# A two-layer block with disentangled attention: SyncE's order of writes and reads of the skewed tables, and tables made 20 slots ahead

## The chip, the cores and the metric

The kernel runs on one core of one Trainium2 chip, as one program. The metric is the device time of one execution in microseconds; the median of the runs counts. TensorE (PE), VectorE (DVE), ScalarE (ACT), GpSimd (POOL) and SyncE (SP) each run their own instruction stream and meet through semaphores. In this kernel SyncE computes nothing; it issues DMAs in the order in which they are written for it.

## The reference

Input x has the shape (4, 1024, 256), float32. Two layers follow each other, each added to its own input after a layer norm:

```
x = x + LN(attention(LN(x)))
x = x + LN(experts(LN(x)))
```

The attention has 16 heads of width 16 and relative positions. With a bucketed distance rel(q, k), clipped to 128 buckets:

```
scores[q,k] = (Q[q].K[k] + Q[q].posK[c2p(q-k)] + K[k].posK[p2c(q-k)]) / sqrt(48)
out = LN(softmax(scores) @ V @ Wo + bo + hidden)
```

The buckets are such that only distances below 128 have a table value of their own; from 128 on, all keys to one side share one value. The second layer sends each token to one of 8 experts (256 to 1024 to 256, ReLU), adding the other experts' constant outputs.

## The kernel before

Five stages run one after the other: `spread` (position tables), `project` (norm, Q, K, V), `attend`, `mix` (output projection, norms, routing) and `experts`. Only `attend` is touched; it takes the time from about 200 us to 1492 us of the span.

**Units and slots.** `attend` works on N = 64 units, one for each batch entry and head. A unit has QT = 8 row tiles of 128 queries; the work on one tile is a slot, counted by s from 0 to 511. All engines walk through the same slots in software-pipelined loops written out by hand; `AHEAD` (16 slots) and `LAG` (13 slots) say how far the first and the last part of a tile's work stand from the score.

**Tables.** For tile x, 16 slots ahead, TensorE's `make_table` (L703) multiplies queries and keys with the head's bucket rows into `table_ps`, a single PSUM buffer; ScalarE's `keep_table` (L852) copies it to `table`. Four tiles make a part (h = 0 for tiles 0 to 3, h = 1 for tiles 4 to 7). SyncE's `skew_write` (L650) writes a part to DRAM (1024 KB), and `skew_read` (L658) reads it back with a row pitch one element shorter, in two DMAs, one for each table (384 KB each for h = 0, 640 KB each for h = 1), so that the value for a distance comes to stand at its key: the tile `near`. The write waits until the fourth table is kept (`table_kept`) and until the reads of the unit two before have landed, as both use the same place in DRAM. The read waits for the landing of its write (`skew_out`) and until the scores of the unit two before have used `near` (`scored`, `seen`).

**Corners.** GpSimd's `edge` (L916) makes the two corner blocks of `near` in five operations for each h (L926, L929, L934, L939, L942), spread over the slots by the tuple `steps` (L964): each entry is (slot in relation to the unit before, h, operations). The last one raises `near_made`. `keep_side` (L910) first copies the last column of the table, which two of the operations use. GpSimd works through its list in order; a wait holds all that stands behind.

**Scores.** TensorE's `score` (L717) makes a 128 x 1024 tile of scores, waits for `near_made`, and adds `near` by transposes (L740). It waits for VectorE's `seen` of two slots ago. VectorE's `look` (L807) takes the maxima and writes the band around the diagonal, `level` (L828, L833) subtracts the running maximum.

**The unit's maximum.** After slot 7 of a unit GpSimd's `split_top` (L947) splits the row maxima in five small operations (L952 to L962); TensorE's `turn_top` (L782, L785), at slot 1 of the next unit, waits for them and turns them into `table_ps`; ScalarE's `keep_top` sends them by DMA to the query tile. The next but one `make_table` waits for `top_kept`.

**The rest of the slot.** 13 slots behind the score, TensorE's `flip` makes the transposed scores in two halves, ScalarE's `exponent` (L865) the exponential, TensorE's `weigh` (L767) the sum with the values.

**SyncE's iteration.** In iteration u of its loop (L677 to L695) SyncE issues, in this order: read(u+1, h=1), write(u+2, h=0), `load_unit(u+4)` (queries and keys in five DMAs, which wait for the flips of unit u-2), store(u-2), read(u+2, h=0), write(u+2, h=1). A batch of values (1152 KB) is loaded at the start and in iterations 4, 20 and 36.

Of the kernel before, what the change touches and what calls it, by code (L numbers as in the profile page):

```python
# [16 lines left out]
P = 128  # L17
# [4 lines left out]
N = B * H  # L22
QT = S // P
# [7 lines left out]
BAND = 2 * P - 1  # L31
# [522 lines left out]

def attend(nc, sem, spent, c_masks, split_d, far_d, v_d, pick_d, skew_d, ctx_d):

    AHEAD = 2 * QT
    LAG = QT + 5
    BUFS = 6
    HATS = 5  # L560
# [13 lines left out]
    with ExitStack() as ctx:  # L574
# [10 lines left out]
        rows = sb("rows", [KROWS, H, 2, 2 * P], BF16)  # L585
        vals = [sb(f"vals{i}", [P, QT, VROW]) for i in range(2)]
        table = [sb(f"table{i}", [P, 2, 2, 4, SPOT]) for i in range(2)]
        side = [sb(f"side{i}", [P, 2, QT]) for i in range(2)]
        near = [sb(f"near{i}", [P, 2, QT, W3]) for i in range(2)]
        band = [sb(f"band{i}", [P, QT, W3]) for i in range(2)]  # L590
        most, peak = sb("most", [P, 2, 2]), sb("peak", [P, 2, 2])
# [36 lines left out]
        @block.sync  # L628
        def _(sp):
            part, far = N * DH * S, PARTS * S  # L630

            def load_unit(n):
                i = n % BUFS
                if n >= BUFS:
                    sp.wait_ge(flipped, 2 * QT * (n - BUFS + 1))
                for dst, side_at in ((after[i], TERMS * part), (quest[i], 0)):
                    sp.dma_start(dst[0:KROWS, :], view(split_d, side_at + n * (DH * S), [[part, TERMS], [S, DH], [1, S]])
                                 ).then_inc(hats_in[i], 16)
                for dst, far_at, many in ((quest[i][FAR:FAR + 6, :], n * (2 * far), 2 * PARTS),
                                          (after[i][KROWS:FAR, :], (N + n) * (2 * far) + far, PARTS),  # L640
                                          (before[i][KROWS:FAR, :], (N + n) * (2 * far), PARTS)):
                    sp.dma_start(dst, view(far_d, far_at, [[S, many], [1, S]])).then_inc(hats_in[i], 16)

            def load_vals(b):
                if b >= 2:
                    sp.wait_ge(summed, QT * BATCH * (b - 1))
                sp.dma_start(vals[b % 2][:, :, :], view(v_d, b * (S * VROW), [[VROW, P], [P * VROW, QT], [1, VROW]])
                             ).then_inc(vals_in[b % 2], 16)

            def skew_write(n, h):  # L650
                sp.wait_ge(table_kept, n * QT + 4 * h + 4)
                if n >= 2:
                    sp.wait_ge(skew_in[n % 2][0], 16 * 2 * (n // 2))
                    sp.wait_ge(skew_in[n % 2][1], 16 * 2 * (n // 2))
                sp.dma_start(view(skew_d, n % 2 * (P * PITCH) + h * 4 * SPOT + 1, [[PITCH, P], [TABLE, 2], [1, 4 * SPOT]]),
                             table[n % 2][:, h, :, :, :].rearrange("p a u v -> p a (u v)")).then_inc(skew_out[n % 2][h], 16)

            def skew_read(n, h):  # L658
                if n >= 2:
                    sp.wait_ge(scored, (n - 2) * QT + 4 * h + 4)  # L660
                    sp.wait_ge(seen, (n - 2) * QT + 4 * h + 4)
                sp.wait_ge(skew_out[n % 2][h], 16 * (n // 2 + 1))
                lo, hi = PIECES[h]
                for tab in range(2):
                    sp.dma_start(near[n % 2][:, tab, lo:hi, P:W3],
                                 view(skew_d, n % 2 * (P * PITCH) + tab * TABLE + lo * SPOT + P,
                                      [[PITCH - 1, P], [SPOT, hi - lo], [1, SPOT]])).then_inc(skew_in[n % 2][h], 16)

            def store(n):
                sp.wait_ge(sum_kept, n + 1)  # L670
                sp.dma_start(view(ctx_d, n * (P * 2 * P), [[2 * P, P], [1, 2 * P]]), made[n % 2][:, :]
                             ).then_inc(ctx_out[n % 2], 16)

            for semaphore in spent:
                sp.sem_clear(semaphore)
            sp.dma_start(rows[:, :, :, :].rearrange("p h a v -> p (h a v)"), pick_d[:, :]).then_inc(rows_in, 16)
            for u in range(-4, N + 3):  # L677
                if 0 <= u + 1 < N:
                    skew_read(u + 1, 1)
                if 0 <= u + 2 < N:  # L680
                    skew_write(u + 2, 0)
                if 0 <= u + 4 < N:
                    load_unit(u + 4)
                if u == -4:
                    sp.dma_start(masks[:, :, :], c_masks).then_inc(const_in, 16)
                if 0 <= u - 2 < N:
                    store(u - 2)
                if u == -4:
                    load_vals(0)
                if u % BATCH == 4 and u // BATCH + 1 < B:  # L690
                    load_vals(u // BATCH + 1)
                if 0 <= u + 2 < N:
                    skew_read(u + 2, 0)
                if 0 <= u + 2 < N:
                    skew_write(u + 2, 1)  # L695
            for i in range(2):
                sp.wait_ge(ctx_out[i], 16 * (N // 2))

        @block.tensor
        def _(pe):  # L700
            ident = masks[:, 4, :]

            def make_table(x):  # L703
                n, u = x // QT, x % QT
                i = n % BUFS
                if u == 0:
                    pe.wait_ge(hats_in[i], 16 * HATS * (n // BUFS + 1))
                if x >= 1:
                    pe.wait_ge(table_kept, x)
                if x >= AHEAD and x % QT == 2:  # L710
                    pe.wait_ge(top_kept, (x - AHEAD) // QT)
                nc.tensor.matmul(table_ps[:, 0, :], quest[i][0:KROWS, u * P:(u + 1) * P], rows[:, n % H, 0, :],  # L712
                                 start=True, stop=False)
                nc.tensor.matmul(table_ps[:, 1, :], after[i][0:KROWS, u * P:(u + 1) * P], rows[:, n % H, 1, :],  # L714
                                 start=False, stop=True).then_inc(table_made, 1)
# [193 lines left out]
        def _(pool):  # L909
            def keep_side(n, h):  # L910
                pool.wait_ge(table_kept, n * QT + 4 * h + 4)
                if n >= 2:
                    pool.wait_ge(edge_made, (n - 2) * 10 + (5 if h == 0 else 10))
                nc.gpsimd.tensor_copy(side[n % 2][:, :, 4 * h:4 * h + 4], table[n % 2][:, h, :, :, BAND]).then_inc(side_kept, 1)

            def edge(n, h, step):  # L916
                i = n % 2
# [6 lines left out]
                if step == 0:  # L924
                    pool.wait_ge(skew_in[i][h], 16 * 2 * (n // 2 + 1))
                    nc.gpsimd.tensor_tensor(head[:, 0, :, :], tail[:, 0, :, :], above, ALU.mult).then_inc(edge_made, 1)  # L926
                elif step == 1:
                    pool.wait_ge(side_kept, n * 2 + h + 1)
                    nc.gpsimd.tensor_tensor(head[:, 1, :, :], tail[:, 1, :, :],  # L929
                                            side[i][:, 1, lo + 1:hi + 1].unsqueeze(2).to_broadcast([P, many, P]),  # L930
                                            ALU.subtract).then_inc(edge_made, 1)
                elif step == 2:
                    pool.wait_ge(edge_made, done + 1)
                    nc.gpsimd.tensor_tensor(tail[:, 0, :, :], tail[:, 0, :, :],  # L934
                                            side[i][:, 0, lo:hi].unsqueeze(2).to_broadcast([P, many, P]),
                                            ALU.subtract).then_inc(edge_made, 1)
                elif step == 3:
                    pool.wait_ge(edge_made, done + 2)
                    nc.gpsimd.tensor_tensor(head[:, 1, :, :], head[:, 1, :, :], above, ALU.mult).then_inc(edge_made, 1)  # L939
                else:  # L940
                    pool.wait_ge(edge_made, done + 3)
                    nc.gpsimd.tensor_tensor(tail, tail, masks[:, 1, :].unsqueeze(1).unsqueeze(1).to_broadcast([P, 2, many, P]),  # L942
                                            ALU.mult).then_inc(edge_made, 1)
                    pool.wait_ge(edge_made, done + 5)
                    pool.sem_inc(near_made, 1)  # L945

            def split_top(n):  # L947
                i, done = n % 2, 5 * n
                if n >= 2:
# [11 lines left out]
                pool.wait_ge(split_made, done + 4)  # L961
                nc.gpsimd.tensor_copy(top_part[i][:, 2, :], top_rest[:, 1, :]).then_inc(split_made, 1)  # L962

            steps = ((2, 0, (0, 1)), (3, 0, (2,)), (4, 0, (3,)), (5, 0, (4,)),  # L964
                     (6, 1, (0, 1)), (7, 1, (2,)), (8, 1, (3,)), (9, 1, (4,)))
            nc.gpsimd.memset(before_rows[:, :], -1.0).then_inc(before_set, 1)
            pool.wait_ge(before_set, 1)
            nc.gpsimd.memset(before_rows[0:6, :], 0.0).then_inc(before_set, 1)
# [2 lines left out]
            pool.wait_ge(const_in, 16)  # L971
            for s in range(-AHEAD, TS):
                u, t = s // QT, s % QT
                if t == 0 and 0 <= u + 1 < N:
                    keep_side(u + 1, 1)
                if t == 4 and 0 <= u + 2 < N:
                    keep_side(u + 2, 0)
                for at, h, of in steps:
                    n = (s - at) // QT + 1
                    if (s - at) % QT == 0 and 0 <= n < N:  # L980
# [659 lines left out]
```

## Time and profile before

| | us |
|---|---|
| median of 3 runs | 2009.08 (2002.75 to 2014.89) |
| the profiled execution | 2003.63 |
| its span, from the first to the last instruction | 2001.7 |
| PE busy / PEld busy | 1698.0 / 1159.6 |
| DVE busy | 1370.7 |
| ACT busy | 1121.8 |
| POOL busy | 1069.1 |
| DMA, mean over the span | 226 GB/s |

The busy times are unions of an engine's instructions. PE is TensorE's matmuls, whose ends are modelled, so that a busy PE is not one at its peak; PEld is its weight loads, which run beside them. A time in brackets behind an instruction is how long its engine stood idle before it, with what ended the idle time.

### The profile page before, as it was taken

The page shows a single profiled execution, that of the slowest core. Times are in us where ns is not written, and L with a number is a line of the kernel's source. Part 1 is how long each engine was busy: PE and PEld are TensorE (multiplying, and loading weights), DVE is VectorE, ACT ScalarE, POOL GpSimd, SP SyncE. Part 2 cuts the span into 40 slices and gives each one's busy share as a digit, 9 for nine tenths or more (in the row PEclk, how much of TensorE's full clock was granted, in tenths as well). Part 3 has the DMA queues.
Part 4 walks back from the last instruction along what each step waited for, and adds up shares of the span by engine and source line. Part 5 has one row for each costly group of instructions (what it writes and reads, how often), then busy time and mean ns, then how long its engine had stood idle before and what let it go on. Part 6 is the DMA issues. An engine that isn't in the chain of part 4 may idle for free. (4 is left out here: it accounts for less than half of the span.)

```text
span 2001.7 us, 40568 instructions
## 1 busy us (share of the span) xinstructions
PE 1698.0 (85%) x13688; PEld 1159.6 (58%) x13688; DVE 1370.7 (68%) x3938; ACT 1121.8 (56%) x2233; POOL 1069.1 (53%) x1268
## 2 busy tenths in 40 slices
PE   1882389999999999999999999999973674999997
PEld 1451156565656566566565666566532464999996
DVE  1673188788888788898798899899843553343343
ACT  1672257676767677677677777677751460222221
POOL 0210267676777667667576777777711451233332
PEclk6996589999999999999999999999996675999998
DMA  4598778777777777777877777787718852676772
GB/s 113 188 303 274 225 250 262 246 237 251 245 261 248 256 247 240 257 254 245 265 237 251 249 261 250 240 272 246 235 44 215 284 176 86 198 212 215 223 219 78
DMA packets 320826, 453.36 MB, mean 226 GB/s; under 512 B 35132, under 2 KB 260303, under 8 KB 320526
## 3 DMA queue, kind: packets, MB, share of 16 engines
q1 hardware_dynamic: 308034, 415.25, 65.2%
q10 hardware_dynamic: 7596, 21.10, 3.4%
q0 software_dynamic: 4992, 14.43, 1.9%
q8 instruction: 112, 1.84, 0.4%
q14 instruction: 92, 0.75, 0.1%
HBM read 257.32 MB, written 193.65 MB: 225 GB/s over the span
## 5 line engine op out<-in xcount | busy, mean ns | idle before, releaser
L865 ACT ACTIVATE t_probsT<-t_flip 128x512 f32<-128x512 f32 x1024 | 619.2, 607 | 242.7 <-PE t_flip L756 117.5
L814 DVE TENSOR_REDUCE t_most<-t_scores 128x1 f32<-128x640 f32 (+1 forms) x512 | 436.7, 853 | 169.8 <-PE t_scores L740 166.5
L833 DVE TENSOR_SCALAR t_band<-t_band,t_top 128x384 f32<-128x384 f32 (+1 forms) x512 | 383.8, 750 | 0.0
L859 ACT COPY t_table<-t_table_ps 128x512 f32<-128x512 f32 x512 | 298.2, 582 | 70.7 <-issue 41.1
L777 PE MATMUL t_sum_ps<-t_probsT,t_vals 128*32 128x256 f32 x4096 | 329.5, 394 | 0.2 <-ACT t_probsT L865 0.2
L926 POOL TENSOR_TENSOR t_near<-t_near,t_masks 128x384 f32<-128x384 f32 (+1 forms) x128 | 146.8, 1147 | 338.9 <-DMA t_near<-skew_d 336.4
L942 POOL TENSOR_TENSOR t_near<-t_near,t_masks 128x768 f32<-128x768 f32 (+1 forms) x128 | 272.4, 2129 | 0.0
L763 PE MATMUL t_flip<-t_masks,t_band 128*128 128x128 f32 x1408 | 263.0, 276 | 0.0
L818 DVE CUSTOM_DVE_ANT_0 t_band<-t_scores,t_near 128x384 f32<-128x384 f32 (+1 forms) x512 | 262.1, 512 | 0.0
L740 PE MATMUL t_scores<-t_masks,t_near 128*128 128x128 f32 x1408 | 243.5, 277 | 7.1 <-POOLq L945 7.1
L733 PE MATMUL t_scores<-t_after,t_quest 105*128 105x256 bf16 (+3 forms) x1024 | 244.9, 289 | 2.6 <-DVE t_most L818 2.4
L740 PEld LDWEIGHTS t_scores<-t_masks,t_near 128*128 128x128 f32 x1408 | 182.7, 143 | 46.6 <-POOLq L945 8.7
L712 PE MATMUL t_table_ps<-t_rows,t_quest 96*128 96x256 bf16 x512 | 143.5, 280 | 69.1 <-DMA t_before<-far_d 49.8
L733 PE MATMUL t_scores<-t_before,t_quest 105*128 105x256 bf16 (+3 forms) x768 | 195.0, 294 | 0.0
L763 PEld LDWEIGHTS t_flip<-t_masks,t_band 128*128 128x128 f32 x1408 | 164.7, 143 | 4.8
L756 PE MATMUL t_flip<-t_quest,t_before 108*128 108x512 bf16 (+3 forms) x512 | 161.4, 316 | 0.8 <-ACT t_probsT L865 0.7
L756 PE MATMUL t_flip<-t_quest,t_after 108*128 108x512 bf16 (+3 forms) x512 | 158.7, 310 | 1.2 <-DMA t_quest<-t_topT 0.8
L1606 PE MATMUL e_hid_ps<-e_xT,e_w 128*128 128x128 f32 x1248 | 148.0, 278 | 5.6 <-DMA e_total<-total_d 5.2
L1606 PEld LDWEIGHTS e_hid_ps<-e_xT,e_w 128*128 128x128 f32 x1248 | 147.5, 194 | 8.2 <-issue 5.5
L939 POOL TENSOR_TENSOR t_near<-t_near,t_masks 128x384 f32<-128x384 f32 (+1 forms) x128 | 145.5, 1137 | 0.0
L714 PE MATMUL t_table_ps<-t_rows,t_after 96*128 96x256 bf16 x512 | 142.9, 279 | 0.0
L1588 PE MATMUL e_out_ps<-w_all,e_hid 128*128 x624 | 141.0, 379 | 0.0
(186 smaller groups left out, 2343.7 us busy)
## 6 DMA issues: line engine op xcount, KB each, us to landing
skew_d<-t_table SPq DMA_DIRECT2D x128, 1024.0 KB, 8.9
t_near<-skew_d SPq DMA_DIRECT2D x128, 640.0 KB, 6.2
t_near<-skew_d SPq DMA_DIRECT2D x128, 384.0 KB, 4.8
e_w<-in_L_ffn_W_dram ACTq DMA_DIRECT2D x39, 512.0 KB
e_w<-in_L_ffn_W_dram SPq DMA_DIRECT2D x39, 512.0 KB
split_d<-p_part SPq DMA_DIRECT2D x32, 384.0 KB
t_after<-split_d SPq DMA_DIRECT2D x64, 192.0 KB
t_quest<-split_d SPq DMA_DIRECT2D x64, 192.0 KB
```

The lines of the kernel that those rows point to most:

```text
L733: nc.tensor.matmul(out[:, at:at + size], quest[i][0:XROWS, t * P:(t + 1) * P], keys[0:XROWS, piece[0] * P:piece[0] * P + size], start=at % ...
L740: last = nc.tensor.matmul(out[:, (j - lo) * P:(j - lo + 1) * P], near[n % 2][:, 1, j, (t - j + 1) * P:(t - j + 2) * P], ident, start=False ...
L756: last = nc.tensor.matmul(out[:, (a - lo) * P:(z - lo) * P], keys[:, j * P:(j + 1) * P], quest[i][:, a * P:z * P], start=first, stop=False ...
L763: last = nc.tensor.matmul(out[:, (t - lo) * P:(t - lo + 1) * P], band[n % 2][:, t, at:at + P], ident, start=False, stop=True, is_transpose ...
L777: last = nc.tensor.matmul(sum_ps[32 * g:32 * g + 32, 0:2 * P], vals[b % 2][:, j, h * VDIM:h * VDIM + 32], probsT[s % 3][:, g * 2 * P:(g + ...
L814: nc.vector.tensor_reduce(most[:, c, 1:2], out[:, wide:S], AX.X, ALU.max)
L818: nc.vector.tensor_tensor_reduce(band[n % 2][:, t, 0:wide], out[:, 0:wide], near[n % 2][:, 0, t, at:at + wide], 1.0, -3.0e38, ALU.add, ALU ...
L833: nc.vector.tensor_scalar(band[n % 2][:, t, 0:wide], band[n % 2][:, t, 0:wide], top[n % 2][:, t:t + 1], None, ALU.subtract).then_inc(level ...
L859: nc.scalar.copy(table[n % 2][:, h, :, u % 4, :], table_ps[:, :, :]).then_inc(table_kept, 1)
L865: nc.scalar.activation(probsT[s % 3][:, half * 512:(half + 1) * 512], flip_ps[half][:, :], ACT.Exp, scale=SCALE).then_inc(expd, 1)
L942: nc.gpsimd.tensor_tensor(tail, tail, masks[:, 1, :].unsqueeze(1).unsqueeze(1).to_broadcast([P, 2, many, P]), ALU.mult).then_inc(edge_made, 1)
L1606: last = nc.tensor.matmul(hid_ps[s % 2][:, c, :], w1[s % WB][:, f, c * P:(c + 1) * P], xT[s % 2][:, f, :], start=(f == 0), stop=(f == 1))
```

## The change

Five edits, all in `attend`:

- SyncE's iteration has a new order: write(u+2, h=0), read(u+1, h=1), `load_unit(u+4)`, write(u+2, h=1), read(u+2, h=0), store(u-2), values.
- `AHEAD` is 20 slots instead of 16, on all engines. TensorE's wait for `top_kept` is kept at the same slot of the unit.
- `side` has three buffers instead of two, and `keep_side` waits for the edges of the unit three before.
- `keep_side` runs four slots earlier in relation to the unit whose column it copies: (u+2, h=0) at slot 0, (u+2, h=1) at slot 4.
- GpSimd's `steps` put each operation of h = 0 and the first three of h = 1 one slot earlier; the fourth and fifth of h = 1 stay at slots 0 and 1 of the next unit and now stand first in a slot.

```diff
-    AHEAD = 2 * QT
+    AHEAD = 2 * QT + QT // 2
...
-        side = [sb(f"side{i}", [P, 2, QT]) for i in range(2)]
+        side = [sb(f"side{i}", [P, 2, QT]) for i in range(3)]
...
             for u in range(-4, N + 3):
+                if 0 <= u + 2 < N:
+                    skew_write(u + 2, 0)
                 if 0 <= u + 1 < N:
                     skew_read(u + 1, 1)
-                if 0 <= u + 2 < N:
-                    skew_write(u + 2, 0)
                 if 0 <= u + 4 < N:
                     load_unit(u + 4)
                 if u == -4:
                     sp.dma_start(masks[:, :, :], c_masks).then_inc(const_in, 16)
+                    load_vals(0)
+                if 0 <= u + 2 < N:
+                    skew_write(u + 2, 1)
+                    skew_read(u + 2, 0)
                 if 0 <= u - 2 < N:
                     store(u - 2)
-                if u == -4:
-                    load_vals(0)
                 if u % BATCH == 4 and u // BATCH + 1 < B:
                     load_vals(u // BATCH + 1)
-                if 0 <= u + 2 < N:
-                    skew_read(u + 2, 0)
-                if 0 <= u + 2 < N:
-                    skew_write(u + 2, 1)
...
-                if x >= AHEAD and x % QT == 2:
+                if x >= AHEAD and (x - AHEAD) % QT == 2:
                     pe.wait_ge(top_kept, (x - AHEAD) // QT)
...
-                if n >= 2:
-                    pool.wait_ge(edge_made, (n - 2) * 10 + (5 if h == 0 else 10))
-                nc.gpsimd.tensor_copy(side[n % 2][:, :, 4 * h:4 * h + 4], table[n % 2][:, h, :, :, BAND]).then_inc(side_kept, 1)
+                if n >= 3:
+                    pool.wait_ge(edge_made, (n - 3) * 10 + 10)
+                nc.gpsimd.tensor_copy(side[n % 3][:, :, 4 * h:4 * h + 4], table[n % 2][:, h, :, :, BAND]).then_inc(side_kept, 1)
...
-            steps = ((2, 0, (0, 1)), (3, 0, (2,)), (4, 0, (3,)), (5, 0, (4,)),
-                     (6, 1, (0, 1)), (7, 1, (2,)), (8, 1, (3,)), (9, 1, (4,)))
+            steps = ((8, 1, (3,)), (9, 1, (4,)), (1, 0, (0, 1)), (2, 0, (2,)), (3, 0, (3,)), (4, 0, (4,)),
+                     (5, 1, (0, 1)), (6, 1, (2,)))
...
-                if t == 0 and 0 <= u + 1 < N:
-                    keep_side(u + 1, 1)
+                if t == 0 and 0 <= u + 2 < N:
+                    keep_side(u + 2, 0)
                 if t == 4 and 0 <= u + 2 < N:
-                    keep_side(u + 2, 0)
+                    keep_side(u + 2, 1)
```

## Rows read from the trace of the kernel before

**Rows 1.** The page, in 40 slices of the span: PE busy tenths, granted clock in tenths.
```profile
PE   1882389999999999999999999999973674999997
...
PEclk6996589999999999999999999999996675999998
```
**Rows 2.** Stretches: length; busy us of PE, PEld, DVE, ACT, POOL; clock; DMA share, GB/s.
```profile
284.50:1440.80 1156.30, 1103.46 (x10137) 694.85 (x10137) 1005.05 (x2881) 841.51 (x1618) 824.56 (x1022) 0.99 0.77 251
1310.40:1346.70 36.30, 36.02 (x343) 22.95 (x338) 33.21 (x98) 28.08 (x54) 26.95 (x35) 1.00 0.78 259
1440.80:1458.40 17.60, 16.63 (x154) 9.83 (x154) 16.56 (x48) 10.34 (x19) 13.60 (x17) 1.00 0.52 177
```
**Rows 3.** Timeline at two turns (L785): start, us, instruction, idle time before it.
```profile
1346.68 0.22 PE L785 MATMUL t_table_ps<-t_ident,t_top_part 128*24 128x128 bf16 x1
...
1458.40 0.23 PE L785 MATMUL t_table_ps<-t_ident,t_top_part 128*24 128x128 bf16 x1 [0.77 <-POOL t_top_part L962]
```
**Rows 4.** TensorE's waits, 284.5 to 1440.8 us: us in total, times, longest.
```profile
PE t_table_ps L785 <- POOL t_top_part L962: 46.3, 46, 4.4
```
**Rows 5.** Timeline of POOL and PE around one late turn; one stretch's clock.
```profile
804.56 1.28 POOL L926 TENSOR_TENSOR t_near<-t_near,t_masks 128x512 f32<-128x512 f32 x1 [5.68 <-DMA t_near<-skew_d]
807.84 0.19 POOL L952 CAST t_top_part<-t_top 128x8 bf16<-128x8 f32 x1
808.91 0.19 POOL L962 CAST t_top_part<-t_top_rest 128x8 bf16<-128x8 f32 x1
809.15 0.23 PE L785 MATMUL t_table_ps<-t_ident,t_top_part 128*24 128x128 bf16 x1 [1.64 <-POOL t_top_part L962]
809.30:812.60 3.30, 3.19 (x19) 2.27 (x22) 0.07 (x1) 1.83 (x4) 3.30 (x2) 0.61 0.86 244
```
**Rows 6.** Timeline of SyncE's queue over one unit.
```profile
1344.78 1.25 SPq L665 DMA_DIRECT2D t_near<-skew_d  x2
1346.13 0.57 SPq L655 DMA_DIRECT2D skew_d<-t_table  x1
1352.66 0.93 SPq L665 DMA_DIRECT2D t_near<-skew_d  x2
1353.69 0.56 SPq L655 DMA_DIRECT2D skew_d<-t_table  x1
...
1357.67 0.36 SPq L671 DMA_DIRECT2D ctx_d<-t_made  x1
1364.10 0.92 SPq L665 DMA_DIRECT2D t_near<-skew_d  x2
```
**Rows 7.** SyncE's own waits, 284.5 to 1440.8 us.
```profile
SPq L662 <- DMA skew_d<-t_table: 702.1, 116, 8.3
```
**Rows 8.** Time to landing of the writes (L655), then of the reads (L665).
```profile
DMA to landing us min/median/max: 5.7/8.9/10.9
...
DMA to landing us min/median/max: 3.7/5.3/8.5
```
**Rows 9.** Timeline of DVE and POOL in the two clean units.
```profile
1327.32 0.35 DVE L833 TENSOR_SCALAR t_band<-t_band,t_top 128x256 f32<-128x256 f32 x1
1329.30 2.37 POOL L942 TENSOR_TENSOR t_near<-t_near,t_masks 128x1024 f32<-128x1024 f32 x1
1329.58 2.23 DVE L833 TENSOR_SCALAR t_band<-t_band,t_top 128x256 f32<-128x256 f32 x1
1343.32 0.08 DVE L825 DVE_READ_ACCUMULATOR t_peak<-t_most 128x1 f32 x1
```
**Rows 10.** Timeline of the start: a table copy, slot 3's wait, the first turn.
```profile
234.81 0.58 ACT L859 COPY t_table<-t_table_ps 128x512 f32<-128x512 f32 x1 [0.70 <-PE t_table_ps L714]
249.27 0.90 PE L740 MATMUL t_scores<-t_masks,t_near 128*128 128x128 f32 x3 [6.90 <-POOLq L945]
265.71 0.28 PE L785 MATMUL t_table_ps<-t_ident,t_top_part 128*24 128x128 bf16 x1 [4.83 <-POOL t_top_part L962]
```
**Rows 11.** DVE's groups, 284.5 to 1440.8 us: busy us, mean ns.
```profile
L833 DVE TENSOR_SCALAR t_band<-t_band,t_top 128x256 f32<-128x256 f32 x480 | 362.0, 754 | 0.0
```

More of the change, by code:

```diff
@@ L929, in edge @@
                     nc.gpsimd.tensor_tensor(head[:, 1, :, :], tail[:, 1, :, :],
-                                            side[i][:, 1, lo + 1:hi + 1].unsqueeze(2).to_broadcast([P, many, P]),
+                                            side[n % 3][:, 1, lo + 1:hi + 1].unsqueeze(2).to_broadcast([P, many, P]),
                                             ALU.subtract).then_inc(edge_made, 1)
@@ L934, in edge @@
                     nc.gpsimd.tensor_tensor(tail[:, 0, :, :], tail[:, 0, :, :],
-                                            side[i][:, 0, lo:hi].unsqueeze(2).to_broadcast([P, many, P]),
+                                            side[n % 3][:, 0, lo:hi].unsqueeze(2).to_broadcast([P, many, P]),
                                             ALU.subtract).then_inc(edge_made, 1)
```

## The prediction

> **What bounds the kernel now.** I read the page's busy shares first [rows 1]. The attention stage runs from about 200 to 1492 us, and there the matmul row sits at nine tenths with a granted clock of nine tenths or more. An average says little here, so I next took one number per unit: the turn of the row maxima (`turn_top`, L785) happens once in each of the 64 units, first at 265.71 us [rows 10]. From the second turn to the 62nd (284.5 to 1440.8) are 60 pitches in 1156.30 us, a mean of 19.27 us [rows 2]. From the turn at 1310.4 to that at 1346.7 are two pitches in 36.30 us, at a full clock, with TensorE busy for 36.02 of them [rows 2], and the turn that ends them shows no idle time before it [rows 3]. So about 18.16 us is what TensorE's own work costs per unit, and about 1.11 us per unit is something else. A slot (one row tile of one head, eight to a unit) is 18.16 / 8 = 2.27 us of it.
>
> The list of waits says what the rest is: before L785 the matmuls waited 46.3 us in 46 places for GpSimd's L962, the last of the five small operations of `split_top` [rows 4]. That is 0.77 us per unit. The rest is a slower clock after such waits: TensorE is busy 1103.46 / 60 = 18.39 us per unit against 18.01 in the two clean ones [rows 2], 0.38 us. Together 1.15 of the 1.11 us. One such place, read across engines [rows 5]: GpSimd sat idle 5.68 us until a read of the skewed table landed, started L926 at 804.56, needed 3.28 us for the three operations ahead of `split_top` and 1.26 us for `split_top`, and TensorE turned at 809.15 after 1.64 us of idleness. After that idle time the granted clock was 0.61 on average from 809.3 to 812.6, so for the greater part its lower level (1.2 GHz) [rows 5]. Both costs are in the 19.27.
>
> Why is the read late? SyncE's queue, over a unit [rows 6]: reads at 1344.78, write at 1346.13, then nothing until 1352.66, reads, write at 1353.69, loads and store to 1358.03, then nothing until 1364.10. Each gap is the wait of the next read for the write just issued. SyncE waited 702.1 us for it in 116 places [rows 7], 11.7 us of each unit. The two round trips in series, 1344.78 to 1364.10, are 19.32 us: they pace the unit, and TensorE is caught by them through GpSimd. A write lands 8.9 us after issue in the median (5.7 to 10.9), a read 5.3 (3.7 to 8.5) [rows 8]. Bandwidth is not what is short: the DMA share is 0.77 at 19.27 us [rows 2].
>
> **The change part by part.** *Order on SyncE and tables 20 slots ahead.* I count in slots from the start of unit u. Before, `skew_write(u+2, 1)` was issued only when SyncE came free at the end of the iteration, and the read of it straight after its landing. Now the two writes of a unit are about half a unit ahead of their reads, with the other write between. The iteration runs: write(u+2,0) at about slot -0.3, when its fourth table is kept; read(u+1,1), after `seen` of unit u-1 (slot 0.7) and the landing of write(u+1,1); `load_unit(u+4)`, which must wait for the flips of unit u-2, slot 4.4 (they run 13 slots late); write(u+2,1); read(u+2,0); store. The wait in `load_unit` is not new, but the write now stands behind it and its five issues. The one chain that can still bind goes from there: on the queue the five loads of `load_unit` take from 1354.25, the end of the write's issue, to 1357.67, 3.4 us [rows 6], the write lands after 8.9, the reads land 8.5 after issue (the largest landing of before, since they now follow a 1 MB write) [rows 8], GpSimd needs 3.28 + 1.26 us [rows 5] until TensorE may turn. That sums to 25.4 us. The turn it feeds stands at slot 18, 13.6 slots after slot 4.4, which at 2.27 us is 30.9 us. So 5.5 us are spare. With the largest write (10.9) and a read longer by another 2.7 us, it is 30.1, still inside. The value batches (1152 KB, three of them in the loop) cost some of that in three units only.
>
> As a rule on the same thing: the Trainium skill, "DMA: Bandwidth & Descriptors", section "Queues, rings and completion order", says that within a queue each DMA engine takes descriptors in ring order. By it a read issued behind a write moves its bytes after it, and reads take longer to land than before while writes take less; the trace of before has the opposite order and fits (write 8.9, read 5.3) [rows 8]. Without the rule one would keep 5.3 for the read, and the spare time would be 8.7 us.
>
> *GpSimd's steps.* The eleven kinds of operation stay as they are, and their number too; 13.7 us of GpSimd per unit (824.56 / 60) [rows 2]. At slot 6 it now does h1's third operation and at slot 7 nothing but `split_top`, so `split_top` starts when slot 7's maximum is there. In the clean unit that maximum was ready at 1343.40 (L825) and the turn stood at 1346.68 [rows 3, 9]: 3.28 us for 1.26 us of work, 2.0 us spare. Behind `split_top` on GpSimd stand the side copy, two h1 operations (L939, taken like L926 at 1.28, and L942 at 2.37 us) [rows 5, 9] and then the h0 chain; h1's `near_made` comes at about 1.26 + 0.2 + 3.65 = 5.1 us after the maximum, some 4 us before slot 3's transposes ask for it. The h0 chain ends near slot 5.5, h1's first three near slot 7.0; GpSimd then idles 18.16 - 13.7 = 4.4 us. Sides in three buffers cost nothing but memory; the operation is the same, and its wait on `edge_made` is for work a unit old.
>
> *Steady gain.* 60 pitches x (19.27 - 18.16) = 66.6 us. The return of the clock is in it, since the two clean pitches are at full clock. The floor may not be held every time: bounds 0 and 0.3 us per unit (the latter a quarter of today's stall); I take 0.06, near the zero that the two adjacent clean units show: -4 us.
>
> *Start.* TensorE makes 20 tables before the first score instead of 16. Each is a round between TensorE and ScalarE of 0.70 + 0.58 = 1.28 us [rows 10], so the first score comes 5.1 us later. But today slot 3 of unit 0 waits 6.90 us for `near_made` of h1 (L740), and the first turn 4.83 us for GpSimd [rows 10]. The 5.1 us lie inside the 6.90. The read that slot 3 waits for no longer waits for read(0,0) to be issued, yet goes behind write(1,0): between -5 and +5 us, I take +1.5. The first turn's 4.83 us goes, as its read has half a unit more. Together 6.3, bounds -5.2 and 11.7.
>
> *End.* The wait of 0.77 us at 1458.40 goes [rows 3]. Four more of the late slots are free of tables; without tables the unit took 17.60 - 0.77 = 16.83 instead of 18.16 [rows 2, 3], so 4 x 0.16 = 0.65. Together 1.4. All other stages are untouched.
>
> Sum: 66.6 - 4 + 6.3 + 1.4 = 70.3 us. The profiled execution took 2003.63 us (span 2001.7): 2003.63 - 70.3 = 1933.3. The median of the three timed runs is 5.4 us above the profiled one; part of that is the scatter of the very stalls that go, so I leave it out of the point and put it in the range.
>
> **The rivals.** *VectorE takes over.* L833 took 0.35 us alone, but 2.23 us where it started during GpSimd's L942 (1329.30 to 1331.67); it ended at 1331.81, just behind it [rows 9]. Its mean is 0.754 [rows 11], so about 0.35 x 8 = 2.8 us of VectorE's 16.75 us per unit (1005.05 / 60) is this waiting. The spare is 18.16 - 16.75 = 1.4 us. GpSimd's operations move against VectorE's slots, so the waiting may grow; if by two thirds, the unit needs 18.64 us and, with slots uneven, about 18.7: 0.54 x 60 = 32 us of the gain is lost, 1966 us. Against it: neither engine has more to do, and in the clean units VectorE was busy 33.21 of 36.30 us without holding TensorE [rows 2]. The Trainium skill has this as a rule, "SBUF — State Buffer", section "Who interferes with whom": a VectorE instruction in a two-port mode and a GpSimd one exclude each other for the whole instruction. The trace agrees in the 2.23 us above.
>
> *The write behind the loads binds (slower).* The chain above must be done in 13.6 slots, so the pitch is at least chain / 1.7. From 32.8 us on, 7.4 more than my sum, the kernel is slower than now. If each of the three transfers in it takes 2.9 us more because three are in the queue at a time, the chain is 34 us, the pitch 20.0, and the time 2003.6 + 60 x 0.73 - 6 = 2041 us. For it: the DMA share must rise to 0.77 x 19.27 / 18.16 = 0.82. Against: the sum of worst landings stays under 31.
>
> *It does not do what it says.* Should GpSimd still start late, because the reads follow a whole write and come at the same point of the unit as now, the pitch stays at 19.27 and only start and end move: about 1998 us, inside 0.5%.
>
> **How the numbers follow.** 0.5% is 10 us, about what a measurement of this kernel can tell from no change. My forecast 0.68, with its own range 1924 to 1948; VectorE 0.18; no effect 0.06; slower 0.08. All of the first two are faster by over 0.5%, and a bit of the third: 0.87. Same 0.06, slower 0.07. The range of 8 in 10: 1923 (no residue, best start) to 1968 (VectorE's case).
>
> **What would show it.** L785's wait for L962 gone or below 5 us in all; pitches of 18.1 to 18.3 us from turn to turn; no stretch of the stage at the lower clock after the first unit; SyncE's wait at L662 for the write reduced to a few us per unit with a new one at L637 for the flips; L665 landing later than 5.3 us, L655 earlier than 8.9; GpSimd idle before L952 (waiting for the maximum) instead of before L926. Wrong, if L740 or L785 waits for GpSimd again, if L814 never waits for scores (VectorE full), or if the first turn is later than 265.7 us.

## The result, and the profile after

The changed kernel takes 1931.18 us in the median of 4 runs (1928.36 to 1933.84), against 2009.65 us (2002.75 to 2014.89): the ratio is 0.9611, 95% interval 0.9579 to 0.9644. The forecast was 1933.0 with a range of 1923 to 1968. The profiled execution took 1933.84 us, span 1931.9, so 69.8 us of span have gone.

The page's slices and the stretches come first, with the columns of [rows 1, 2]. The lines of the file have moved: L785 is now L783, GpSimd's L952 is L950, L962 is L960, L926 is L924, L740 is L738.

```profile
PE   1883289999999999999999999999944774999997
...
PEclk6897579999999999999999999999976665999999
```

```profile
281.50:1370.30 1088.80, 1080.11 (x10132) 687.90 (x10128) 1003.36 (x2879) 839.70 (x1614) 831.15 (x1020) 1.00 0.85 265
1370.30:1931.90 561.60, 443.93 (x2918) 381.24 (x2913) 238.54 (x818) 163.10 (x445) 183.40 (x187) 0.84 0.58 175
```

The first stretch is again from the second turn to the 62nd: 60 pitches in 1088.80 us where there were 1156.30 [rows 2]. All but two of them are 18.16 or 18.17 us, one is 18.37, and the last, without tables, is 16.88. The granted clock is 1.00 instead of 0.99, so the returns to 1.2 GHz that followed the waits [rows 5] are gone too. The second stretch is all that follows; before, it took 560.9 us from the 62nd turn. The 69.8 us are made up of 3.0 before the second turn (284.5 to 281.5), 67.5 in the pitches, and -0.7 behind them. Between the two medians lie 78.5 us; the kernel before scattered over 12.1 us in its four runs, the changed one over 5.5.

Next the waits of all engines from 277 to 1372 us (total, times, longest); these lines answer to [rows 4].

```profile
POOL t_top_part L950 <- DVE t_peak L823: 209.0, 60, 4.1
PEld t_flip L754 <- ACT t_probsT L863: 115.8, 302, 0.4
...
DVE t_most L812 <- PE t_scores L738: 66.9, 203, 0.4
...
POOL t_near L924 <- DMA t_near<-skew_d: 14.1, 11, 3.9
...
PEld t_flip L754 <- DMA t_quest<-t_topT: 2.3, 5, 0.6
...
PEld t_table_ps L783 <- POOL t_top_part L960: 0.2, 1, 0.2
```

GpSimd now waits for the maximum, 3.5 us per unit. Its wait for the read of the table, which had held it 5.68 us in the unit of [rows 5], is down to 14.1 us in 11 places. The turn waits for nobody, but for 0.2 us before one weight load. SyncE's own waits over the whole run follow, which answer to [rows 7], and then the landing times of the writes and of the reads [rows 8].

```profile
SPq L637 <- PE t_flip L761: 423.1, 58, 7.7
...
SPq L662 <- DVE t_most L816: 54.8, 51, 5.2
...
SPq L662 <- DMA skew_d<-t_table: 19.9, 15, 5.3
```

```profile
DMA to landing us min/median/max: 5.3/7.5/12.6
...
DMA to landing us min/median/max: 4.6/7.9/14.5
```

The wait of a read for its write fell from 702.1 us to 19.9. Reads now land later (7.9 against 5.3) and writes sooner (7.5 against 8.9), and neither shows up before the turn. Last, the timeline of SyncE's queue and of GpSimd over one unit, with the turn that ends it:

```profile
1304.92 0.76 SPq L637 DMA_DIRECT2D t_after<-split_d  x1
...
1307.72 0.56 SPq L655 DMA_DIRECT2D skew_d<-t_table  x1
1308.40 1.64 SPq L665 DMA_DIRECT2D t_near<-skew_d  x2
1310.08 1.28 SPq L671 DMA_DIRECT2D ctx_d<-t_made  x1
1312.34 0.56 SPq L655 DMA_DIRECT2D skew_d<-t_table  x1
1314.04 1.78 SPq L665 DMA_DIRECT2D t_near<-skew_d  x2
...
1325.01 1.29 POOL L924 TENSOR_TENSOR t_near<-t_near,t_masks 128x512 f32<-128x512 f32 x1 [0.22 <-DMA t_near<-skew_d]
1327.25 1.16 POOL L932 TENSOR_TENSOR t_near<-t_near,t_side 128x512 f32<-128x512 f32 x1
1332.52 0.25 POOL L950 CAST t_top_part<-t_top 128x8 bf16<-128x8 f32 x1 [4.11 <-DVE t_peak L823]
1333.66 0.19 POOL L960 CAST t_top_part<-t_top_rest 128x8 bf16<-128x8 f32 x1
1335.28 0.22 PE L783 MATMUL t_table_ps<-t_ident,t_top_part 128*24 128x128 bf16 x1
```

This is the one chain that the prediction said could still bind: loads from 1304.92, write at 1307.72, the reads of it at 1314.04, GpSimd at 1325.01, turn at 1335.28. Its slack can be read off: GpSimd idles 4.11 us ahead of `split_top`, and between the end of `split_top` (1333.85) and the turn are another 1.4 us. That is 5.5 us, the figure that was worked out. This unit has the longest of GpSimd's 60 waits for the maximum; with their mean of 3.5 us the slack is 4.9.

### The profile page after: what moved, and what is told of

It is laid out like the page before. It is cut to its first block and busy times, and to the rows that moved or that the text cites. A ratio compares the mean times of both kernels' runs of the same rounds, so it can differ in the third digit from the quotient of the medians.

```text
span 1931.9 us, 40507 instructions
## 1 busy us (share of the span) xinstructions
PE 1683.3 (87%) x13688; PEld 1156.0 (60%) x13688; DVE 1371.6 (71%) x3938; ACT 1122.5 (58%) x2233; POOL 1076.7 (56%) x1268
## 5 line engine op out<-in xcount | busy, mean ns | idle before, releaser
L831 DVE TENSOR_SCALAR t_band<-t_band,t_top 128x384 f32<-128x384 f32 (+1 forms) x512 | 387.7, 757 | 0.0
L940 POOL TENSOR_TENSOR t_near<-t_near,t_masks 128x768 f32<-128x768 f32 (+1 forms) x128 | 271.4, 2120 | 0.0
L738 PE MATMUL t_scores<-t_masks,t_near 128*128 128x128 f32 x1408 | 241.7, 275 | 1.4 <-POOLq L943 1.3
L738 PEld LDWEIGHTS t_scores<-t_masks,t_near 128*128 128x128 f32 x1408 | 181.9, 143 | 40.8 <-POOLq L943 2.5
L924 POOL TENSOR_TENSOR t_near<-t_near,t_masks 128x384 f32<-128x384 f32 (+1 forms) x128 | 147.8, 1155 | 41.8 <-DMA t_near<-skew_d 21.7
L754 PE MATMUL t_flip<-t_quest,t_before 108*128 108x512 bf16 (+3 forms) x512 | 159.8, 314 | 0.8 <-ACT t_probsT L863 0.7
L754 PE MATMUL t_flip<-t_quest,t_after 108*128 108x512 bf16 (+3 forms) x512 | 158.2, 309 | 0.3
L937 POOL TENSOR_TENSOR t_near<-t_near,t_masks 128x384 f32<-128x384 f32 (+1 forms) x128 | 146.0, 1141 | 0.0
```

The source lines that it names most:

```text
L738: last = nc.tensor.matmul(out[:, (j - lo) * P:(j - lo + 1) * P], near[n % 2][:, 1, j, (t - j + 1) * P:(t - j + 2) * P], ident, start=False ...
L754: last = nc.tensor.matmul(out[:, (a - lo) * P:(z - lo) * P], keys[:, j * P:(j + 1) * P], quest[i][:, a * P:z * P], start=first, stop=False ...
L831: nc.vector.tensor_scalar(band[n % 2][:, t, 0:wide], band[n % 2][:, t, 0:wide], top[n % 2][:, t:t + 1], None, ALU.subtract).then_inc(level ...
```

## The experiments

Twelve kernels were run. "Before" in each group is the kernel before on the same chip: 2016.53 us for e1 to e4, 2013.26 for e5 to e8, 2016.27 for e9 to e12. Pitches are means of 60 from the second turn (L785 or L783) to the 62nd, in the profiled execution of each. The 19.27 us of the kernel before belong to an execution of 2003.63 us; the 12.9 us by which its median on the chip of e1 to e4 is longer would make about 19.5 (an estimate, if they are spread over the 64 units).

### Which part of the change does it

**e1: the order undone, the rest kept.**

```diff
-                if 0 <= u + 2 < N:
-                    skew_write(u + 2, 0)
                 if 0 <= u + 1 < N:
                     skew_read(u + 1, 1)
+                if 0 <= u + 2 < N:
+                    skew_write(u + 2, 0)
...
-                if 0 <= u + 2 < N:
-                    skew_write(u + 2, 1)
-                    skew_read(u + 2, 0)
                 if 0 <= u - 2 < N:
                     store(u - 2)
...
+                if 0 <= u + 2 < N:
+                    skew_read(u + 2, 0)
+                if 0 <= u + 2 < N:
+                    skew_write(u + 2, 1)
```

> The changed kernel with one part undone: SyncE's iteration has the old order again (read h1, write h0, loads, store, read h0, write h1); tables stay 20 slots ahead, as do side's three buffers and GpSimd's list. Theory A (the series of write, landing, read on SyncE paces a unit, whatever the tables do): the pitch from turn to turn goes back to 19.1 to 19.5 us, SyncE waits some 700 us at L662 for landings, L785 waits for GpSimd again, the time is 1990 to 2012 us. Rival B (what counts is that the tables are there half a unit sooner): the pitch stays at 18.2 to 18.4 us and the time at 1931 to 1945 us.

Measured: ratio 1.0025 (1.0006 to 1.0044) to the kernel before, 2021.83 us, pitch 19.60. SyncE and TensorE wait as they did (300 to 1400 us of this kernel):

```profile
PE t_table_ps L785 <- POOL t_top_part L962: 59.9, 49, 4.8
```

```profile
SPq L662 <- DMA skew_d<-t_table: 690.4, 112, 8.8
```

Theory A holds and rival B falls: tables that are there four slots sooner are of no use to an order that issues each write only after the wait for the one before it.

**e2: the order alone.** The kernel before, with the new loop body and nothing else.

> The kernel before with SyncE's new order alone; tables are still 16 slots ahead and GpSimd's list is the old one. Theory A with the order of events: write h0 now waits until the fourth table is kept, slot 3.7 of the unit, and read h1 stands behind it. From there 0.5 us of issue, 10.9 us to landing (as in the changed kernel), 3.4 us of GpSimd and 1.3 us of split_top make 16.1 us against the 6.3 slots or 14.3 us until the turn: 1.8 us of waiting at L785 in every unit, a pitch of 20.0 us, 2045 us, up to 2100 if the clock falls after each wait. Rival C (the order alone breaks the series and is enough): 1931 to 1950 us. A pitch near 19.3 would say that neither part alone changes anything.

Measured: ratio 1.0062 (1.0037 to 1.0086), 2030.43 us, pitch 19.85. SyncE does not wait for its writes to land; it waits for tables:

```profile
SPq L655 <- ACT t_table L857: 563.4, 111, 10.1
```

```profile
PE t_table_ps L783 <- POOL t_top_part L960: 72.2, 56, 2.6
```

Rival C falls. The forecast of 1.8 us of waiting per unit was too much, 76.4 us over the 60 turns are 1.3, and so was 2045 us; place and sign were right. Both parts are needed: the order lets a write go as soon as its tables are kept, and 20 slots make them be kept in time.

**e3: could GpSimd's order alone have done it?** The kernel before, with `split_top` ahead of the h1 operations.

```diff
-                     (6, 1, (0, 1)), (7, 1, (2,)), (8, 1, (3,)), (9, 1, (4,)))
+                     (8, 1, (0, 1)), (8, 1, (2,)), (8, 1, (3,)), (9, 1, (4,)))
```

> The kernel before with one edit on GpSimd: the first three operations of h1's edges stand behind split_top instead of ahead of it, so that the turn no longer waits for the read of the table. Theory A (SyncE's series of round trips paces the unit at 19.3 us, and the turn is only where TensorE feels it): L785's wait goes, the same time turns up at L740 for near_made, pitch 19.0 to 19.5 us, time 1990 to 2015 us. Rival D (only GpSimd's order caught TensorE): pitch 18.2 to 18.5 us, 1935 to 1955 us.

Measured: ratio 1.0054 (1.0036 to 1.0073), 2027.14 us, pitch 19.59, a little above the forecast of 19.0 to 19.5. TensorE's and SyncE's waits, 300 to 1400 us:

```profile
PE t_scores L740 <- POOLq L945: 66.9, 56, 2.9
```

```profile
SPq L662 <- DMA skew_d<-t_table: 653.5, 111, 8.3
```

The turn waits for nothing, and the same time stands at the transposes of slot 3. This is what makes "SyncE's two round trips pace the unit" more than a reading: the place where TensorE feels them can be moved, the time cannot. Nor does the slower clock set the pace: in e3's 60 pitches the granted clock was 1.00, and they were no shorter.

**e11: GpSimd's numbers undone.** The changed kernel with the old tuple `steps`.

> The changed kernel with the old numbers in GpSimd's tuple steps. GpSimd has no clock of slots: it works down a list, and with the old numbers the list of a unit is the same but for one side copy of 0.2 us, which stands ahead of L937 instead of behind it. Theory A: no change, 1928 to 1936 us, no wait at L783. Rival H (moving the operations one slot earlier was needed to free slot 7 for split_top, as the prediction's text put it): waits at L783, 1940 us or more.

Measured: ratio 0.9578 (0.9562 to 0.9594), 1932.2 us, pitch 18.16, no idle time before any turn. Laid side by side, GpSimd's list of a unit with the old numbers differs by one side copy of 0.2 us, ahead of L937 instead of behind it. Rival H, which is the prediction's own sentence on slot 7, falls.

### How much there is to spare

**e4: the loads behind the write.**

```diff
-                if 0 <= u + 4 < N:
+                if 0 <= u + 4 < N and u < 0:
                     load_unit(u + 4)
...
                     skew_write(u + 2, 1)
                     skew_read(u + 2, 0)
+                if 0 <= u + 4 < N and u >= 0:
+                    load_unit(u + 4)
```

> The changed kernel with load_unit moved behind write h1 and read h0 from unit 0 on, so that the write no longer stands behind the wait for the flips and behind five issues. Theory A (the chain load, write, read, GpSimd has 5 to 6 us to spare): no change in time, 1927 to 1936 us, pitch 18.16 us; the write is issued about a slot or two sooner, GpSimd's idle time for the maximum stays 3 to 4 us per unit. Rival E (the write behind the loads costs something in some units): the time falls by 3 us or more.

Measured: 1931.09 us, ratio 0.9569 (0.9547 to 0.9591), pitch 18.14. GpSimd waited 216.8 us for the maximum (3.6 per unit) and 1.8 for reads. The place behind the loads costs nothing.

**e5, e6, e7: the write held back**, by a wait on scored slots, with nothing else moved and no byte added.

```diff
                 if 0 <= u + 2 < N:
+                    if u >= 0:
+                        sp.wait_ge(scored, u * QT + 7)   # 8 in e6, 9 in e7
                     skew_write(u + 2, 1)
```

> The changed kernel with one more wait on SyncE: write h1 of unit u+2 waits until slot 6 of unit u is scored (7 slots; it is issued at slot 5.9 without it). It measures how much the chain has to spare. Working: from the anchor the write lands in 7.5 us, the read in 10.9, GpSimd needs 3.4 and split_top 1.3, with issues 23.7 us; the turn that it feeds is one turn plus 6 slots and more away: pitch P from 2P = 5 slots x 2.27 + 23.7 = 35.0, so 17.5 us, below TensorE's 18.16. Theory A: no change, 1928 to 1937 us. Rival F (the spare time is less than 3 us): L785 waits again and the time is above 1945 us.

> As the one before, with the wait for 8 slots scored. 2P = 6 slots x 2.27 + 23.7 = 37.3 us, so a pitch of 18.65 us instead of 18.16: theory A gives 1931 + 60 x 0.49 = 1960 us (1935 to 1985), with a first few tenths of waiting at L785 per unit. If the spare time is over 8 us: no change, 1931 us.

> As the one before, with the wait for 9 slots scored. 2P = 7 slots x 2.27 + 23.7 = 39.6 us, a pitch of 19.8 us: theory A gives 1931 + 60 x 1.64 = 2029 us (2005 to 2060), slower than the kernel before although its order of DMAs and its tables are those of the changed kernel. If a later write cost nothing because reads would only be issued a little later: 1931 us.

| kernel | pitch forecast | pitch | us | ratio (interval) | idle before the 60 turns |
|---|---|---|---|---|---|
| e5, 7 slots | 18.16 | 18.37 | 1944.96 | 0.9658 (0.9634 to 0.9682) | 0.0 |
| e6, 8 slots | 18.65 | 19.13 | 1991.56 | 0.9881 (0.9859 to 0.9903) | 7.1 |
| e7, 9 slots | 19.8 | 19.85 | 2036.11 | 1.0116 (1.0072 to 1.0161) | 48.6 |

e7 is slower than the kernel before: a write some three slots (7 us) late spends the whole gain. The prediction's slower rival was a real mechanism, and its price of 2041 us was near. But e5 and e6 were missed, and e7's number is in part luck: its matmuls waited 45.8 us at the turn, and 26.2 us for the transfer that the forecast had left out and that the next lines show. With a write held by one slot 14 us went, and the turn did not wait at all. TensorE's waits, from 300 to 1400 us, e5 first, then e6:

```profile
PE t_flip L756 <- DMA t_quest<-t_topT: 10.7, 21, 1.5
```

```profile
PE t_flip L756 <- DMA t_quest<-t_topT: 41.6, 51, 1.6
PE t_table_ps L785 <- POOL t_top_part L962: 7.1, 3, 2.8
```

**e8: tables 18 slots ahead.** Two tables fewer before the first score; the side copies at slots 2 and 6.

> The changed kernel with tables 18 slots ahead instead of 20 and the two side copies two slots later. At the start two tables fewer are made before the first score, 2 x 1.28 = 2.6 us. In the loop write h0 comes two slots later (slot 1.7 of the next unit instead of 7.9 of this one) and read h1 behind it 2.8 us later, which the 5.9 us to spare should cover. Theory A: pitch 18.16 us, 1928 to 1933 us. Rival: the spare time is used up, L785 waits, 1940 us or more.

Measured: 1939.64 us, ratio 0.9625 (0.9604 to 0.9646), pitch 18.30. Missed, and by the same wait: L754 waited 6.4 us in 14 places for `t_topT`, its weight loads 32.6 us in 58, and no turn of the 60 waited. At the start the first score did come 2.5 us sooner (VectorE's first maximum at 241.45 instead of 243.92), but slot 3's transposes then waited until 250.05, and the second turn came at 280.6 instead of 281.5, which is within the scatter of the start (below).

**e9, e10: is it a second deadline?** The turned maxima go by a DMA of 6 KB on ScalarE's queue into the query tile, and the unit's first flip, three slots after the turn, needs them. In e6 (timelines of SyncE, TensorE and ScalarE):

```profile
1050.66 0.55 SPq L655 DMA_DIRECT2D skew_d<-t_table  x1
1052.66 1.30 SPq L665 DMA_DIRECT2D t_near<-skew_d  x2
...
1051.84 0.22 PE L785 MATMUL t_table_ps<-t_ident,t_top_part 128*24 128x128 bf16 x1
...
1052.41 0.73 ACTq L879 DMA_DIRECT2D t_quest<-t_topT  x1
...
1060.12 0.28 PE L756 MATMUL t_flip<-t_quest,t_after 108*128 108x256 bf16 x1 [1.00 <-DMA t_quest<-t_topT]
```

The turn is on time at 1051.84. The 6 KB are issued at 1052.41, beside 1.0 MB of write and 1.3 MB of reads. Their last packet ends 6.4 us later, and the flip starts 7.7 us after the issue. In the changed kernel that flip starts 6.6 us after the issue (median), so the transfer, with what passes between its last packet and the flip (1.3 us here), has no more time than that. Its last packet ended 5.1 us after the issue there, 6.0 in e5 and 6.1 in e6 (medians of 60, from the packets in the traces). In e4, where the loads stand behind the bulk, it ended after 3.7. To tell this from the table chain, all flips were put one slot later:

```diff
-    LAG = QT + 5
+    LAG = QT + 6
```

> The kernel with write h1 held until 7 slots are scored (1945 us against 1931), and beside it LAG 14 instead of 13: every flip, exponential and sum stands one slot later. In the profile of the held write GpSimd was never late (no wait at L785), but the first flip of a unit waited 12.8 us in 28 units for the 6 KB DMA of the row maxima (t_quest<-t_topT), whose last packet ends 5.96 us after its issue in the median, against 5.07 in the changed kernel. Theory G (a second deadline: the small DMA queues behind the bulk writes and reads that are now issued just ahead of it, and the flips three slots after the turn catch it): with a slot more, pitch back to 18.16 to 18.2 us, 1931 to 1937 us. Rival F (the 14 us come from the table chain itself): pitch stays 18.35 to 18.4, 1943 to 1950 us.

> The kernel with write h1 held until 8 slots are scored (1991.6 us, pitch 19.13), with LAG 14. Theory G: the 44.5 us of waits for the small DMA in 55 units go; what remains is the table chain, for which a pitch of 18.65 was worked out (18.2 to 18.8), now with waits at L785: 1935 to 1970 us. Rival F: it stays at 1985 to 1995 us, the wait only changes its place.

Measured: e9 1932.05 us, ratio 0.9585 (0.9569 to 0.9601), pitch 18.11; e10 1942.71 us, ratio 0.9635 (0.9619 to 0.9651), pitch 18.35. The waits for `t_topT` are gone from both, but for 0.4 us before one weight load in e9, and e9's only wait of TensorE's matmuls in 300 to 1400 us is this:

```profile
PE t_table_ps L785 <- POOL t_top_part L962: 1.3, 3, 0.5
```

Theory G holds. One slot of lag gives back 13 of the 14 us that e5 had lost against the changed kernel, and 49 of e6's 60. In e10 the table chain binds a little (9.2 us in 7 places before turns), less than the 18.65 us of pitch that was worked out. The lag alone, without the held write, was not run: e9's commonest pitch is 18.11 us against 18.16 or 18.17 in the changed kernel, so some 3 us of each gain may be the lag's own.

### What bounds a unit now

**e12: part of the value sums left out.**

```diff
-                for g in range(4):
+                for g in (range(4) if j in (0, QT - 1) else range(2)):
                     last = nc.tensor.matmul(sum_ps[32 * g:32 * g + 32, 0:2 * P], ...
```

> The changed kernel with 12 of the 32 column groups of the value sums left out in each unit (two of four groups in slots 1 to 6); all else is as it was. It asks what bounds a unit now. Theory I (TensorE's own work is the 18.16 us): a group costs 0.16 us and more, so 1.9 to 3 us less per unit, until VectorE, busy 16.8 us of each unit, holds it: pitch 16.9 to 17.2 us, 1855 to 1875 us, with waits of L731 for VectorE's L816. Rival J (something else with the same period, ScalarE's exponentials or the DMAs, is already at 18.16): the pitch stays at 18.0 to 18.2 us.

Measured: 1928.36 us, ratio 0.9563 (0.9546 to 0.9579), pitch 18.07. The numbers are rival J's, but the experiment doesn't decide, since its premise was wrong. A slot with two groups, and one with four:

```profile
704.45 0.62 PE L775 MATMUL t_sum_ps<-t_probsT,t_vals 128*32 128x256 f32 x4
...
706.64 0.64 PE L775 MATMUL t_sum_ps<-t_probsT,t_vals 128*32 128x256 f32 x8
```

Half the matmuls take almost the same time: from their start to the start of what follows are 0.558 us with two groups and 0.572 with four (medians, from the starts in the traces). So the edit took at most 0.1 us per unit from TensorE's path. The pitch did fall by about as much: 56 of its 60 are 18.06 or 18.07 us, where 18.16 and 18.17 stood before. That fits theory I better than rival J, on an effect too small to carry it. What sets the 18.16 us stays open. That it is TensorE's own work is a reading: it is busy 1080.11 of 1088.80 us at full clock, and from 277 to 1372 us its matmuls show no wait for another engine. But its weight loads for L754 show gaps of up to 0.4 us put down to ScalarE (115.8 us in 302 places, in the list of waits above), and no run here took those away.

## Why the prediction was right, step by step

**SyncE's series as the pace: right, shown.** e1 has the changed kernel's tables and the old time. e3 moves the wait from one place to another, and the time stays within 0.6%.

**The sum as a whole: right, and closer than its terms.** It gave 70.3 us, and 69.8 of span went. The pitches gave 67.5 where 62.6 and the end's 1.4 were put, 3.5 more; the start gave 3.0 instead of 6.3, 3.3 less; and behind the 62nd turn 0.7 went the other way (1.0 gained up to the 64th, 1.7 lost behind it, 529.8 us against 528.1). That these nearly cancel is luck. The forecast also started from the profiled execution (2003.63 us) and not from the median, 5.4 us above it, in part because the scatter of the stalls would go. The scatter did shrink, from 12.1 us to 5.5, and the changed kernel's median lies 1.8 us below the forecast; with so few runs that is no proof of the reason.

**The steady gain, 66.6 - 4 us, with 1.4 at the end: right.** Measured are 67.5 us from turn to turn, the end's 1.3 us in the last pitch among them. The residue of 0.06 us per unit was not needed: the two clean units had shown the floor exactly, and 58 of 60 pitches stand on it.

**The chain behind the loads, 5.5 us to spare: right in the sum, wrong in two of its terms.** The read was taken at 8.5 us and the write at 8.9. The profiled unit shows 10.97 us from the reads' issue to GpSimd's start. The write's landing is mostly not what releases the reads: 51 waits for VectorE's `seen` stand against 15 for landings, and in this unit the read is issued 6.3 us after its write. The two errors cancel. e7 shows the price when the slack is gone, e4 that the loads' place costs nothing.

**GpSimd's steps: wrong, without a consequence in the sum.** The prediction said that slot 7 is now free for `split_top` because the operations stand one slot earlier. GpSimd knows no slots: it goes down a list, and the list is the same but for one copy (e11). What made `split_top` punctual is the read that lands in time.

**The start, 6.3 us: mis-sized.** The first turn came at 263.84 instead of 265.71, 1.9 us sooner, and the second 3.0. The first score was later by the four tables, as said (VectorE's first maximum at 243.92 against 238.73). But slot 3 waited until 249.75, where it had waited until 249.27 [rows 10], so the +1.5 us for the read was -0.5. The 4.83 us at the turn could not all be had either: where it waits for no read (the changed kernel, e2 and e3), the first turn comes 3.0 us after VectorE starts slot 7's maximum. Before, that maximum started at 258.45, so the turn could have come at about 261.4. From slot 3 on VectorE held the unit. The timeline of the changed kernel's start:

```profile
247.25 2.54 DVE L831 TENSOR_SCALAR t_band<-t_band,t_top 128x256 f32<-128x256 f32 x1
...
247.29 2.35 POOL L940 TENSOR_TENSOR t_near<-t_near,t_masks 128x1024 f32<-128x1024 f32 x1
...
249.75 0.55 PE L738 MATMUL t_scores<-t_masks,t_near 128*128 128x128 f32 x3 [1.27 <-POOLq L943]
...
257.85 0.91 PE L731 MATMUL t_scores<-t_after,t_quest 105*128 105x256 bf16 x3 [1.79 <-DVE t_most L816]
```

VectorE's `level` met GpSimd's longest operation and ran until just behind it, as in [rows 9]; without overlap this form took 0.35 us there. The rule of the Trainium skill that the prediction weighed ("SBUF — State Buffer", section "Who interferes with whom") fits this too: VectorE's 247.25 lies inside the GpSimd operation before (L937, 246.07 to 247.34), and VectorE came free 0.15 us behind L940. In the start of this execution such meetings cost VectorE some 2 us: VectorE began slot 3's maximum at 251.79 instead of 250.21 and slot 7's at 260.84 instead of 258.45, while slot 3's transposes were only 0.5 us later. That the four tables moved the scores onto GpSimd's operations is an inference. It also depends on the execution: in those of e4, e5, e6, e7, e11 and e12, whose kernels start the stage the same way but for one side copy in e11, the first turn came between 262.01 and 263.20, against 263.84 here. The forecast's 6.3 us would have put it near 259.4, and none came so early. In the loop it cost nothing more than before: the mean of L831 is 755 ns against 754 [rows 11], and VectorE is busy 16.7 us of 18.16. The VectorE rival did not come.

**What the prediction did not see** is the second deadline of e5, e6 and e8, the 6 KB DMA behind the turn. In the changed kernel it is just met (2.3 us of weight-load waits in the whole stage). The sum with its 5.5 us of slack was true for the turn, but a kernel that used one slot of it already lost 14 us elsewhere (e5).

## What to carry to other kernels

When one queue issues a write, waits for it to land and issues the read of it, the round trips add up to a period of their own; compare that sum with the pitch before looking at the engine that seems to be waited for. To take them apart, a queue needs the next write's data early as well as its place ahead of the read: either alone gave nothing here. Slack worked out for one deadline holds for that one alone; list each small transfer that shares the engines with the bulk, and its first user, before spending it.

## What was not expected of the hardware

- A DMA of 6 KB on ScalarE's queue served its first user only 7.7 us after its issue (e6), with 1.0 MB of write and 1.3 MB of reads issued within 1.8 us of it. Its last packet ended 3.7 us after the issue in e4, 5.1 in the changed kernel, 6.0 in e5 and 6.1 in e6 (medians). The last 1 us of that cost up to 13 us over the kernel (e5) and up to 49 (e6); these are what a slot more of lag gave back. That it waits behind bulk packets in the shared engines is inferred from when the bulk is issued; the runs show only that it is late and that a later first use cures it.
- Four value-sum groups of 32 columns each take 0.64 us together and two take 0.62 (e12), and what follows starts after 0.57 or 0.56 us. The groups, which go to different quarters of the output partitions, overlap in time. Leaving two of four out frees next to nothing.
- Reads issued right behind a write of 1 MB landed after 7.9 us in the median instead of 5.3, and the writes after 7.5 instead of 8.9, while the DMA share rose from 0.77 to 0.85 for nearly the same bytes per unit (251 x 19.27 us = 4.84 MB, 265 x 18.15 us = 4.81 MB). So the share multiplied by the pitch rose by 4% (14.8 to 15.4 us): the same bytes kept the DMA engines busy a little longer. Why is not shown.
